# A recommendation kernel: one table fetched by single rows on two queues, weight loads spread between them, and a reordered tail

## The chip, the cores and the metric

The kernel runs on one core of one Trainium2 chip. Its time is device microseconds for one execution: a median of 236.08 us over three runs (235.92 to 236.24). The engines are PE (TensorE), DVE (VectorE), ACT (ScalarE), POOL (GpSimd) and SP (SyncE), and all transfers run on 16 DMA engines.

## The reference

For 512 samples, each of 26 tables (6250 rows of 128 float32) gives one row. The rows are summed, and they also feed a three-layer network:

```python
emb = jax.vmap(lambda tab, idx: tab[idx])(tables, cat_features)      # 26 x 512 x 128
emb_btd = jnp.transpose(emb, (1, 0, 2))
wide_num = jax.nn.relu(numerical @ w_wide + b_wide)                  # 13 numbers per sample
linear_output = jnp.sum(emb_btd, axis=1) + wide_num
x = jnp.concatenate([numerical, emb_btd.reshape(512, 26 * 128)], axis=1)
x = jax.nn.relu(x @ W1 + b1)                                         # 3341 -> 256
x = jax.nn.relu(x @ W2 + b2)                                         # 256 -> 128
return jax.nn.sigmoid(x @ W3 + b3 + linear_output)                   # 512 x 128
```

## The kernel before

A *tile* (t, c) is the 128 rows that table t gives for chunk c of 128 samples, four chunks in all. Every engine runs a list written out by hand, and semaphores tie the lists together. Tiles reach SBUF (`emb`) in three ways:

- **POOL** gathers most of them: `gather` (L299) is one indirect DMA for one tile. There are 97.
- **Rows apart.** SP fetches tiles (0, 2) and (0, 3), and ACT fetches tile (0, 1), row by row: `load_places` (L251) loads 32 row addresses into registers, `fetch_row` (L256) is one MOVE and one DMA of 512 bytes. SP does this in one go, after its four loads of W1 (L269). ACT does four rows in each step i of its loop (L622), which waits until part i is transposed (`turned`) and also loads a piece of table 12.
- **Table 12** is not gathered. It is read whole, in 13 pieces (`load_piece`, L243), as 49 blocks. For each block DVE marks which samples want which row (`hot_block`, L526), and PE multiplies block by marks into one bank (`pick_block`, L369).

The body of the work goes by 46 *parts*. A part is one table for two chunks. For part i PE transposes two tiles (`turn_part`, L344), DVE copies the result to SBUF (L546) and adds it to the running sum (L553), and PE multiplies it by W1 (`sum_part`, L358). PE's list has turn i+1, the blocks of step i, sum i. Table 0 is late: part 36 is (0, 0) with (0, 2), and part 43 is (0, 1) with (0, 3). Two parts stand behind it. In the float32 matmuls (L358, L369) one product is two passes on PE; a transpose is one. So a part is 2 passes of transposes, 4 of sums, and about 2.3 of blocks.

The tail treats tables 23 and 24 tile by tile (eight tiles, n = 0 to 7): PE transposes (L412), ACT copies (L633), DVE adds to the running sum (L587), PE multiplies by W1 (L421), and for each chunk follow the relus, layer 2 (L436), the turned running sum (`begin_total`, L431), layer 3 (L444), and the sigmoid (L642). `small_products` (L384, L387) are the 13-number part and the transposed biases. They stand behind part 1's sum, and the first picked block waits for them.

Of the kernel before, what the change touches and what calls it, by code (L numbers as in the profile page):

```python
# [11 lines left out]
P = 128  # L12
# [4 lines left out]
BY_SCALAR = [(0, 1)]  # L17
REGS = 32
ROWS_A_STEP = 4
# [3 lines left out]
W1_CUTS = [0, 2, 8, 17, 26]  # L23


def build(nc, num, cat, tables, w_wide, b_wide, W1, b1, W2, b2, W3, b3, out):
# [21 lines left out]
    assert all(t == 0 for t, c in BY_SYNC + BY_SCALAR)  # L48
# [8 lines left out]
    PICK_PARTS = (2, LAST - 8)  # L57
# [6 lines left out]
    def blocks(i):  # L64
        lo, hi = PICK_PARTS
        return range((i - lo) * BLOCKS // (hi - lo), (i + 1 - lo) * BLOCKS // (hi - lo)) if lo <= i < hi else range(0)
# [4 lines left out]
    BODY_TILES = [(0, 0)] + [tile for i in range(LAST) for tile in tiles(i) if tile != (0, 0) and not rows_apart(*tile)]  # L71

    assert BODY_TILES[1] == (1, 0)

# [10 lines left out]
    with ctx:  # L85
# [25 lines left out]
        def total_of(c):  # L111
            return total[c % 2][:, 0:D]
# [12 lines left out]
        next_sum = sb("next_sum", [P, 1])  # L125
# [52 lines left out]
        wide_cols, vec_place = total[0][:, 0:CH], total[0][:, CH:CH + KH + 2]  # L178
# [44 lines left out]
        late_gathered = [sem(f"late_gathered{n}") for n in range(TILES)]  # L223
        late_turned = sem("late_turned")
# [38 lines left out]
        def _(sp):  # L263
            with nc.allow_non_contiguous_dma(reason="one index for each partition"):
                sp.dma_start(first_cat[:, :], cat[0:1, 0:P].rearrange("a p -> p a")).then_inc(first_loaded, 16)
                sp.dma_start(next_cat[:, :], cat[1:2, 0:P].rearrange("a p -> p a")).then_inc(next_loaded, 16)
            for i, loaded in enumerate(w1_loaded):
                lo, hi = W1_CUTS[i], W1_CUTS[i + 1]
                sp.dma_start(w1[:, lo:hi, :], W1[NUM + lo * D:NUM + hi * D, :].rearrange("(t d) n -> d t n", d=D)  # L269
                             ).then_inc(loaded, 16)  # L270
# [16 lines left out]
        def _(gp):  # L287
# [18 lines left out]
            gather(0, 0, first_row[:, :], gathered[part_of(0, 0)])  # L306
            gp.wait_ge(next_steps, 4)
            gather(1, 0, next_row[:, :], gathered[part_of(1, 0)])
# [8 lines left out]
        def _(pe):  # L317
# [44 lines left out]
            def pick_block(j):  # L362
                if j == 0:
                    pe.wait_ge(vecs_ready, 1)
# [27 lines left out]
            turn_part(0)  # L392
            for i in range(LAST):
# [6 lines left out]
                if i == PICK_PARTS[0] - 1:  # L400
                    small_products()
# [3 lines left out]
            def turn_tile(n):  # L405
# [4 lines left out]
                else:  # L410
                    pe.wait_ge(late_added, n - 1)
# [28 lines left out]
            def layer3(c):  # L440
                pe.wait_ge(h2_ready, c + 1)
                if c == 0:
# [6 lines left out]
            for c in range(CH):  # L449
                n = c * LATE  # L450
                turn_tile(n)
                if c == 0:
                    sum_part(LAST - 1)
                else:
                    sum_tile(n - 1)
                    begin_total(c - 1)
                if c >= 2:
                    layer3(c - 2)
                turn_tile(n + 1)
                sum_tile(n)  # L460
                if 1 <= c < CH - 1:
                    layer2(c - 1)
            sum_tile(TILES - 1)
            layer2(CH - 2)
            layer2(CH - 1)
            layer3(CH - 2)
            begin_total(CH - 1)
# [3 lines left out]
        def _(dve):  # L471
# [3 lines left out]

            dve.wait_ge(first_loaded, 16)
            nc.vector.tensor_scalar(first_lim[:, :], first_cat[:, :], float(-V), float(V - 1), ALU.max, ALU.min
# [4 lines left out]
            nc.vector.tensor_tensor(first_row[:, :], first_neg[:, :], first_lim[:, :], ALU.add  # L482
                                    ).then_inc(first_steps, 1)
# [6 lines left out]
            nc.vector.tensor_scalar(next_lim[:, :], next_cat[:, :], float(-V), float(V - 1), ALU.max, ALU.min  # L490
# [6 lines left out]
            nc.vector.tensor_tensor(next_sum[:, :], next_neg[:, :], next_lim[:, :], ALU.add).then_inc(next_steps, 1)  # L497
            dve.wait_ge(next_steps, 3)
            nc.vector.tensor_scalar(next_row[:, :], next_sum[:, :], float(V), None, ALU.add).then_inc(next_steps, 1)
# [40 lines left out]
            for j in blocks(PICK_PARTS[0]):  # L540
                hot_block(j)
            for i, (_, q) in enumerate(PARTS):
# [12 lines left out]
                if i == PICK_PARTS[0] - 1:  # L555
                    small_steps()
                if i >= PICK_PARTS[0]:
                    for j in blocks(i + 1):
                        hot_block(j)
                if i == PICK_PARTS[1] - 1:  # L560
# [119 lines left out]
```

## Time and profile before

| | |
|---|---|
| median of three runs | 236.08 us |
| the profiled execution's own time | 237.66 us |
| its span, first to last instruction | 235.9 us |
| PE / DVE / ACT / POOL busy | 126.2 / 76.9 / 6.2 / 93.1 us |
| mean granted TensorE clock | 0.841 |
| DMA packets, bytes | 11244, 14.06 MB |

Busy time counts no DMA issue, register load or semaphore, so SP, which only issues, shows none. "q" behind an engine's name (SPq, ACTq) is that engine's instruction queue. In the slices each digit is the busy share of 5.9 us. A chain of waits is followed back from the last instruction; "issue" in it is time for which the profile shows no releaser.

### The profile page before, as it was taken

What the parts mean: (1) busy time and instruction counts of PE and PEld (TensorE: products, weight loads), DVE (VectorE), ACT (ScalarE), POOL (GpSimd) and SP (SyncE); (2) the same over time, 40 slices, a digit from 0 to 9 for tenths busy, and PEclk for the clock granted to TensorE, in tenths of its full rate; (3) what the DMA queues carried; (4) which work ended last, traced back from release to release, by engine and by line L of the source; (5) the groups of instructions that cost most, each with busy time, mean ns of one, the idle gap of its engine ahead of it and who ended that gap; (6) DMA issues with size and microseconds to landing.
All of it is one profiled execution on the core that took longest, in us unless ns stands there. A gap on an engine that the chain in (4) does not pass through costs nothing.

```text
span 235.9 us, 2252 instructions
## 1 busy us (share of the span) xinstructions
PE 126.2 (54%) x476; PEld 82.6 (35%) x476; DVE 76.9 (33%) x182; ACT 6.2 (3%) x18; POOL 93.1 (39%) x106
## 2 busy tenths in 40 slices
PE   2638200059000700060002719999999999999695
PEld 0415100034000300030002206666666666667594
DVE  3150000033000200110003018677667666845352
ACT  0200000000000000000000000000000000000052
POOL 5777777777777777777771000000000000000000
PEclk9999999999855555575555667999999999999999
DMA  5997613565545443362422003400000000000001
GB/s 150 331 262 170 106 47 51 52 47 103 54 61 45 103 57 48 52 97 54 52 54 63 5 2 93 138 9 4 4 5 4 2 2 1 2 6 2 1 13 34
DMA packets 11244, 14.06 MB, mean 60 GB/s; under 512 B 3308, under 2 KB 8015, under 8 KB 11231
## 3 DMA queue, kind: packets, MB, share of 16 engines
q0 software_dynamic: 3104, 6.36, 20.7%
q1 hardware_dynamic: 4768, 3.80, 5.4%
q10 hardware_dynamic: 3359, 3.76, 5.2%
q8 instruction: 4, 0.07, 0.1%
q14 instruction: 9, 0.07, 0.1%
HBM read 13.65 MB, written 0.26 MB: 59 GB/s over the span
## 4 chain that ended last, share of the span: by engine, by line
SPq 57%; issue 34%; PE 5%; DMA 1%; DVE 1%; ACT 0%; DVEq 0%
SPq L256 50%; SPq L251 7%; PE first_layer L358 1%; PE first_layer L421 1%; DMA first_cat<-in_r_cat_features 1%; PE first_layer L436 1%; PE total L444 1%; DMA emb<-in_L_rec_tables 0%; PE total L431 0%; PE turn L412 0%; PE turn L344 0%; ACT y L642 0%; PE total L320 0%; DVE row_idx L503 0%; DVE cat_row L495 0%
## 5 line engine op out<-in xcount | busy, mean ns | idle before, releaser
L299 POOL DMA_INDIRECT emb<-in_L_rec_tables,row_idx x95 | 89.7, 944 | 29.0 <-issue 29.0
L358 PE MATMUL first_layer<-emb_t,w 128*128 128x256 f32 x184 | 54.4, 423 | 68.2 <-issue 61.3
L358 PEld LDWEIGHTS first_layer<-emb_t,w 128*128 128x128 f32 x184 | 37.6, 212 | 94.4 <-issue 81.8
L369 PE MATMUL total<-hot,block_rows 128*128 128x512 f32 (+1 forms) x98 | 53.8, 656 | 24.8 <-issue 24.8
L546 DVE COPY emb_t<-turn 128x256 f32<-128x256 f32 x46 | 19.4, 422 | 105.4 <-remote 78.3
L526 DVE TENSOR_SCALAR hot<-total,row_no 128x512 f32<-128x512 f32 x49 | 35.3, 742 | 0.0
L369 PEld LDWEIGHTS total<-hot,block_rows 128*128 128x128 f32 (+1 forms) x98 | 17.5, 211 | 32.0 <-issue 32.0
L344 PE MATMUL turn<-ident,emb 128*128 128x128 f32 x92 | 20.3, 304 | 9.0 <-DMA emb<-in_L_rec_tables,row_idx 5.5
L344 PEld LDWEIGHTS turn<-ident,emb 128*128 128x128 f32 x92 | 13.9, 156 | 16.3 <-DMA emb<-in_L_rec_tables,row_idx 6.6
L553 DVE TENSOR_TENSOR emb_sum<-turn,emb_sum 128x256 f32<-128x256 f32 x44 | 18.3, 415 | 0.0
L533 DVE TENSOR_SCALAR wide<-total,b_sb 128x4 f32<-128x4 f32 x1 | 0.2, 222 | 31.6 <-issue 31.6
L633 ACT COPY late_t<-turn 128x128 f32<-128x128 f32 x8 | 2.1, 264 | 219.2 <-PE turn L412 219.2
L421 PE MATMUL first_layer<-late_t,w 128*128 128x128 f32 x32 | 5.0, 280 | 0.1
L421 PEld LDWEIGHTS first_layer<-late_t,w 128*128 128x128 f32 x32 | 4.2, 191 | 0.4 <-ACT late_t L633 0.2
L334 PE MATMUL first_layer<-num_t,w_num 13*128 13x256 f32 x8 | 3.8, 649 | 0.8 <-DVE num_t L509 0.8
L587 DVE TENSOR_TENSOR emb_sum<-turn,emb_sum 128x128 f32<-128x128 f32 x8 | 2.3, 292 | 3.0 <-ACT late_t L633 2.9
L334 PEld LDWEIGHTS first_layer<-num_t,w_num 13*128 13x128 f32 x8 | 2.5, 325 | 1.8 <-DVE num_t L509 1.3
L513 DVE TENSOR_SCALAR pick_lim<-pick_cat 128x512 f32<-128x512 int32 x1 | 0.4, 427 | 7.6 <-DMA pick_cat<-in_r_cat_features 7.6
L320 PE MATMUL total<-ident,cat_row 104*128 104x104 f32 x1 | 0.4, 408 | 4.0 <-DVE cat_row L495 4.0
L436 PE MATMUL first_layer<-h,w 128*128 128x128 f32 x16 | 2.3, 278 | 0.0
L412 PE MATMUL turn<-ident,emb 128*128 128x128 f32 x8 | 2.2, 272 | 0.0
L436 PEld LDWEIGHTS first_layer<-h,w 128*128 128x128 f32 x16 | 2.1, 191 | 0.0
(54 smaller groups left out, 34.2 us busy)
## 6 DMA issues: line engine op xcount, KB each, us to landing
emb<-in_L_rec_tables SPq DMA_DIRECT2D x256, 0.5 KB
block_rows<-in_L_rec_tables ACTq DMA_DIRECT2D x12, 256.0 KB, 2.9
w<-in_L_rec_W SPq DMA_DIRECT2D x2, 1152.0 KB
emb<-in_L_rec_tables ACTq DMA_DIRECT2D x128, 0.5 KB
emb<-in_L_rec_tables,row_idx POOLq DMA_INDIRECT x95
w<-in_L_rec_W SPq DMA_DIRECT2D x1, 768.0 KB
w<-in_L_rec_W SPq DMA_DIRECT2D x1, 256.0 KB
pick_cat<-in_r_cat_features ACTq DMA_DIRECT2D x1, 256.0 KB
```

Source lines behind the costliest of these rows:

```text
L251: eng.load(regs, cat_byte[t * CH + c:t * CH + c + 1, lo:lo + REGS])
L256: eng.dma_start(emb[b:b + 1, t, c, :].bitcast(U8), row_bytes[t:t + 1, bass.ds(at, ROW)]).then_inc(fetched[t, c], 16)
L299: nc.gpsimd.indirect_dma_start(emb[:, t, c, :], None, rows, bass.IndirectOffsetOnAxis(ap=index, axis=0)).then_inc(landed, 16)
L334: nc.tensor.matmul(first_half(k, q), w1_num[:, chunk(k)], cols, start=True, stop=True)
L344: mm = nc.tensor.transpose(turn[i % 2][:, chunk(j)], emb[:, t, c, :], ident[:, :])
L358: mm = nc.tensor.matmul(first_half(k, q), w1[:, t, chunk(k)], emb_t[:, i % SLOTS, :], start=False, stop=False, skip_group_check=True)
L369: mm = nc.tensor.matmul(pick_bank[:, :], block_rows[0:n, j, :], hot[0:n, j % PICK_RING, :], start=(j == 0), stop=(j == PER))
L421: mm = nc.tensor.matmul(first_chunk(k, c), w1[:, LATE_TABLES[g], chunk(k)], late_t[:, n, :], start=False, stop=False, skip_group_check=True)
L436: mm = nc.tensor.matmul(second_chunk(c), w2[:, k, :], h1[:, k, chunk(c)], start=False, stop=False, skip_group_check=True)
L526: nc.vector.tensor_scalar(hot[:, j % PICK_RING, :], pick_row[:, :], row_no[:, j:j + 1], None, ALU.is_equal).then_inc(hot_ready, 1)
L546: nc.vector.tensor_copy(emb_t[:, i % SLOTS, :], turn[i % 2][:, 0:HW]).then_inc(copied, 1)
L553: nc.vector.tensor_tensor(emb_sum[:, q, :], turn[i % 2][:, 0:HW], emb_sum[:, q, :], ALU.add).then_inc(added, 1)
```

## The change

- ACT also fetches tile (0, 0): 256 rows on ACT, 256 on SP, 96 gathers on POOL. ACT's rows no longer wait for `turned`. It loads two pieces of table 12 before them and one more ahead of each 18 rows.
- W1 is loaded in nine DMAs instead of four: two (tables 0 to 4) at SP's start, one ahead of each of SP's first seven register loads.
- POOL begins with tiles (1, 0) and (1, 2), which together are part 0.
- `small_products` stand behind part 0's transposes, in another bank. Two picked blocks are done before part 1, and blocks go along from part 0 on.
- Part (0, 1) is the last of the 46.
- In the tail the body's sums of all four chunks are transposed together, before the first tile's product (`begin_totals`), and DVE adds the late tiles to them as they were gathered, without waiting for the transposes.

```diff
-BY_SCALAR = [(0, 1)]
+BY_SCALAR = [(0, 0), (0, 1)]
-ROWS_A_STEP = 4
+ROWS_A_PIECE = 18
+PIECES_AHEAD = 2
+BLOCKS_AHEAD = 2
-W1_CUTS = [0, 2, 8, 17, 26]
+W1_CUTS = [0, 2, 5, 8, 11, 14, 17, 20, 23, 26]
+W1_AHEAD = 2
-    PARTS += [(t, q) for t in OTHERS[-4:-1] for q in range(2)] + [(0, 1)]
-    PARTS += [(t, q) for t in OTHERS[-1:] for q in range(2)]
+    PARTS += [(t, q) for t in OTHERS[-4:] for q in range(2)] + [(0, 1)]
...
-    PICK_PARTS = (2, LAST - 8)
+    PICK_PARTS = LAST - 8
...
-            for i, loaded in enumerate(w1_loaded):
+            for i in range(W1_AHEAD):
+                load_w1(i)
+            cuts = iter(range(W1_AHEAD, len(w1_loaded)))
             sp.wait_ge(bytes_ready, 1)
             for t, c in BY_SYNC:
                 for lo in range(0, P, REGS):
+                    for i in itertools.islice(cuts, 1):
+                        load_w1(i)
                     regs = load_places(sp, t, c, lo)
...
+                if i == 1:
+                    pe.wait_ge(vecs_ready, 1)
...
             turn_part(0)
+            small_products()
+            for j in range(BLOCKS_AHEAD):
+                pick_block(j)
...
-            def begin_total(c):
-                pe.wait_ge(late_added, (c + 1) * LATE)
-                if c >= 2:
-                    pe.wait_ge(y_ready, c - 1)
-                nc.tensor.matmul(total_of(c), sum_chunk(c), ident[:, :], start=True, stop=False, skip_group_check=True)
+            def begin_totals():
+                pe.wait_ge(added, LAST)
+                for c in range(CH):
+                    mm = nc.tensor.matmul(total_of(c), sum_chunk(c), ident[:, :], start=(c < 2), stop=False,
+                                          skip_group_check=True)
+                mm.then_inc(totals_begun, 1)
...
             def add_tile(n):
                 c, g = divmod(n, LATE)
-                dve.wait_ge(late_copied, n + 1)
+                dve.wait_ge(totals_begun, 1)
+                if c >= 2:
+                    dve.wait_ge(y_ready, c - 1)
...
+                dve.wait_ge(late_gathered[n], 16)
+                nc.vector.tensor_tensor(total_of(c), total_of(c), emb[:, LATE_TABLES[g], c, :], ALU.add
...
+            for i in range(PIECES_AHEAD):
+                load_piece(act, i)
...
-            for i in range(LAST):
-                act.wait_ge(turned, i + 1)
-                if i < PIECES:
-                    load_piece(act, i)
-                for t, c, b in places[i * ROWS_A_STEP:(i + 1) * ROWS_A_STEP]:
-                    if b % REGS == 0:
-                        regs = load_places(act, t, c, b)
-                    fetch_row(act, regs.pop(0), t, c, b)
+            for i, (t, c, b) in enumerate(places):
+                piece, apart = divmod(i, ROWS_A_PIECE)
+                if apart == 0 and piece + PIECES_AHEAD < PIECES:
+                    load_piece(act, piece + PIECES_AHEAD)
+                if b % REGS == 0:
+                    regs = load_places(act, t, c, b)
+                fetch_row(act, regs.pop(0), t, c, b)
```

SP's list from its first instruction, before; w is W1, first_cat and next_cat are the indices of the first two gathers:

```order
L265 DMA first_cat<-in_r_cat_features 128x1
L266 DMA next_cat<-in_r_cat_features 128x1
L269 DMA w<-in_L_rec_W 128x2x256
L269 DMA w<-in_L_rec_W 128x6x256
L269 DMA w<-in_L_rec_W 128x9x256 x2
L251 TENSOR_LOAD cat_byte
L256 DMA emb<-in_L_rec_tables 1x512 x32
```

and in the changed kernel:

```order
L268 DMA first_cat<-in_r_cat_features 128x1
L269 DMA next_cat<-in_r_cat_features 128x1
L273 DMA w<-in_L_rec_W 128x2x256
L273 DMA w<-in_L_rec_W 128x3x256 x2
L254 TENSOR_LOAD cat_byte
L259 DMA emb<-in_L_rec_tables 1x512 x32
L273 DMA w<-in_L_rec_W 128x3x256
```

Eight of the 26 tables of W1 are now ahead of the first row; the other 18 come in six loads, one after each 32 rows.

ACT's list around its first rows, before (block_rows is a piece of table 12, cat_byte the row addresses):

```order
L614 DMA pick_cat<-in_r_cat_features 128x512
L617 ACT_TABLE_LOAD
L617 ACTIVATE table_warm<-ident 1x1
L243 DMA block_rows<-in_L_rec_tables 128x512
L251 TENSOR_LOAD cat_byte
L256 DMA emb<-in_L_rec_tables 1x512 x4
L243 DMA block_rows<-in_L_rec_tables 128x512
```

and in the changed kernel:

```order
L246 DMA block_rows<-in_L_rec_tables 128x512 x2
L636 ACT_TABLE_LOAD
L636 ACTIVATE table_warm<-ident 1x1
L246 DMA block_rows<-in_L_rec_tables 128x512
L254 TENSOR_LOAD cat_byte
L259 DMA emb<-in_L_rec_tables 1x512 x18
L246 DMA block_rows<-in_L_rec_tables 128x512
L259 DMA emb<-in_L_rec_tables 1x512 x14
```

Before, four rows stood behind each piece, and each piece behind a wait for `turned`. Now ACT's rows wait for nothing but the addresses.

PE's list from the last part's sum into the tail, before (late_t is a copied late tile, h the hidden layer):

```order
L358 MATMUL first_layer_1<-emb_t,w 128x256 x2
L412 MATMUL turn<-ident,emb 128x128
L421 MATMUL first_layer_0<-late_t,w 128x128 x2
L412 MATMUL turn<-ident,emb 128x128
L421 MATMUL first_layer_0<-late_t,w 128x128 x2
L431 MATMUL total<-ident,emb_sum 128x128
```

and in the changed kernel:

```order
L371 MATMUL first_layer_1<-emb_t,w 128x256 x2
L445 MATMUL total<-ident,emb_sum 128x128 x4
L435 MATMUL first_layer_0<-late_t,w 128x128 x2
L426 MATMUL turn<-ident,emb 128x128 x2
L435 MATMUL first_layer_0<-late_t,w 128x128 x2
L435 MATMUL first_layer_1<-late_t,w 128x128 x2
```

The four transposes of the sums (L445) now stand in front of the tail's first product. Before, one (L431) stood in each chunk's work.

## Rows read from the trace of the kernel before

**Rows 1.** The page's slices.

```profile
PE   2638200059000700060002719999999999999695
...
POOL 5777777777777777777771000000000000000000
PEclk9999999999855555575555667999999999999999
```

**Rows 2.** The chain that ended last, by line, from the page.

```profile
SPq L256 50%; SPq L251 7%; PE first_layer L358 1%; PE first_layer L421 1%; DMA first_cat<-in_r_cat_features 1%; PE first_layer L436 1%; PE total L444 1%; DMA emb<-in_L_rec_tables 0%; PE total L431 0%; PE turn L412 0%; PE turn L344 0%; ACT y
```

**Rows 3.** The chain in order of time: start us, us, what.

```profile
34.06 0.71 SPq L256
34.77 0.69 issue
...
75.50 0.70 SPq L251
...
140.96 0.23 SPq L256
141.19 0.04 issue
...
143.19 2.18 SPq L251
155.89 2.12 SPq L251
...
219.24 1.18 DMA emb<-in_L_rec_tables
```

**Rows 4.** DVE's timeline, 49 to 128 us: start, us, operation, idle before.

```profile
49.56 0.22 DVE L533 TENSOR_SCALAR wide<-total,b_sb 128x4 f32<-128x4 f32 x1 [31.62 <-issue]
55.11 0.42 DVE L546 COPY emb_t<-turn 128x256 f32<-128x256 f32 x1 [3.61 <-issue]
76.95 0.42 DVE L546 COPY emb_t<-turn 128x256 f32<-128x256 f32 x1 [19.77 <-remote]
99.49 0.43 DVE L546 COPY emb_t<-turn 128x256 f32<-128x256 f32 x1 [21.13 <-remote]
127.62 0.42 DVE L546 COPY emb_t<-turn 128x256 f32<-128x256 f32 x1 [26.73 <-remote]
```

**Rows 5.** PE's timeline, single stretches.

```profile
24.24 0.24 PE L387 MATMUL total<-ident,vec_rows 4*128 4x4 f32 x1
53.48 0.64 PE L344 MATMUL turn<-ident,emb 128*128 128x128 f32 x2
140.91 2.08 PE L358 MATMUL first_layer<-emb_t,w 128*128 128x256 f32 x4 [6.89 <-DVE emb_t L546]
144.69 1.03 PE L358 MATMUL first_layer<-emb_t,w 128*128 128x256 f32 x4
220.47 0.33 PE L344 MATMUL turn<-ident,emb 128*128 128x128 f32 x1 [2.50 <-DMA emb<-in_L_rec_tables]
```

**Rows 6.** ACT's timeline.

```profile
7.12 0.20 ACT L617 ACTIVATE table_warm<-ident 1x1 f32<-1x1 f32 x1
...
27.77 9.09 ACTq L256 DMA_DIRECT2D emb<-in_L_rec_tables  x4
55.10 0.37 ACTq L243 DMA_DIRECT2D block_rows<-in_L_rec_tables  x1
55.56 1.21 ACTq L256 DMA_DIRECT2D emb<-in_L_rec_tables  x4
```

**Rows 7.** ACT's loads of 32 addresses (L251): ns min/median/max, first and last start.

```profile
L251 ACTq TENSOR_LOAD <-cat_byte x4: 2133/2160/2253, 14.1 to 177.5; - x4
```

**Rows 8.** POOL's timeline, the second gather and the last.

```profile
4.98 0.94 POOL L299 DMA_INDIRECT emb<-in_L_rec_tables,next_row  x1 [0.30 <-issue]
123.70 0.94 POOL L299 DMA_INDIRECT emb<-in_L_rec_tables,row_idx  x1 [0.30 <-issue]
```

**Rows 9.** The chain from the last row on: start us, us, what.

```profile
221.88 0.87 PE first_layer L358 x4
224.92 0.45 PE first_layer L421 x4
225.98 0.22 PE total L431 x2
```

**Rows 10.** DMA packets in 0 to 20, 0 to 80 and 0 to 140.3 us.

```profile
DMA packets 5425, 4.85 MB, mean 243 GB/s; under 512 B 1294, under 2 KB 5006, under 8 KB 5425
DMA packets 7685, 9.19 MB, mean 115 GB/s; under 512 B 2198, under 2 KB 5955, under 8 KB 7682
DMA packets 9228, 12.16 MB, mean 87 GB/s; under 512 B 2861, under 2 KB 6649, under 8 KB 9225
```

More of the change, by code:

```diff
@@ L1 @@
+import itertools
 from contextlib import ExitStack
@@ L43, in build @@
     assert LATE == 2 and B == CH * P and D == P and H2 == P and KH == 2 and T * CH <= P and W1_CUTS[-1] == T
-    assert all(t == 0 for t, c in BY_SYNC + BY_SCALAR)
+    assert sorted(BY_SYNC + BY_SCALAR) == [(0, c) for c in range(CH)]
     OTHERS = [t for t in range(1, T) if t not in LATE_TABLES and t != PICK_TABLE]
     PARTS = [(t, q) for t in OTHERS[:-4] for q in range(2)] + [(0, 0)]
-    PARTS += [(t, q) for t in OTHERS[-4:-1] for q in range(2)] + [(0, 1)]
-    PARTS += [(t, q) for t in OTHERS[-1:] for q in range(2)]
+    PARTS += [(t, q) for t in OTHERS[-4:] for q in range(2)] + [(0, 1)]
     LAST = len(PARTS)
     assert HALF == 2 and LAST == (BODY - 1) * 2 and PARTS[0][1] == 0 and PARTS[1][1] == 1
-    PICK_PARTS = (2, LAST - 8)
+    PICK_PARTS = LAST - 8
     PICK_END = LAST - 7
@@ L64, in blocks @@
     def blocks(i):
-        lo, hi = PICK_PARTS
-        return range((i - lo) * BLOCKS // (hi - lo), (i + 1 - lo) * BLOCKS // (hi - lo)) if lo <= i < hi else range(0)
+        n = BLOCKS - BLOCKS_AHEAD
+        return range(BLOCKS_AHEAD + i * n // PICK_PARTS, BLOCKS_AHEAD + (i + 1) * n // PICK_PARTS) if i < PICK_PARTS else range(0)
     def rows_apart(t, c):
         return (t, c) in BY_SYNC + BY_SCALAR
-    BODY_TILES = [(0, 0)] + [tile for i in range(LAST) for tile in tiles(i) if tile != (0, 0) and not rows_apart(*tile)]
-    assert BODY_TILES[1] == (1, 0)
+    BODY_TILES = [tile for i in range(LAST) for tile in tiles(i) if not rows_apart(*tile)]
+    assert BODY_TILES[:2] == [(1, 0), (1, 2)]
     def part_of(t, c):
@@ L305, in _ @@
             gp.wait_ge(first_steps, 3)
-            gather(0, 0, first_row[:, :], gathered[part_of(0, 0)])
-            gp.wait_ge(next_steps, 4)
-            gather(1, 0, next_row[:, :], gathered[part_of(1, 0)])
+            gather(1, 0, first_row[:, :], gathered[part_of(1, 0)])
+            gp.wait_ge(next_steps, 3)
+            gather(1, 2, next_row[:, :], gathered[part_of(1, 2)])
             gp.wait_ge(rows_ready, 1)
@@ L441, in layer3 @@
                 pe.wait_ge(h2_ready, c + 1)
+                pe.wait_ge(late_added, (c + 1) * LATE)
                 if c == 0:
@@ L453, in _ @@
                     sum_part(LAST - 1)
+                    begin_totals()
                 else:
+                    if c >= 2:
+                        layer3(c - 2)
                     sum_tile(n - 1)
-                    begin_total(c - 1)
-                if c >= 2:
-                    layer3(c - 2)
+                sum_tile(n)
                 turn_tile(n + 1)
-                sum_tile(n)
-                if 1 <= c < CH - 1:
+                if c >= 1:
                     layer2(c - 1)
             sum_tile(TILES - 1)
-            layer2(CH - 2)
             layer2(CH - 1)
             layer3(CH - 2)
-            begin_total(CH - 1)
             layer3(CH - 1)
@@ L538, in small_steps @@
                 nc.vector.tensor_scalar(w3_wide[:, :], ones[:, :], w3_col, None, ALU.mult).then_inc(w3_ready, 1)
-            for j in blocks(PICK_PARTS[0]):
+            for j in range(BLOCKS_AHEAD):
+                hot_block(j)
+            small_steps()
+            for j in blocks(0):
                 hot_block(j)
@@ L554, in _ @@
                                             ).then_inc(added, 1)
[L555 to L560, printed above, removed]
+                for j in blocks(i + 1):
+                    hot_block(j)
+                if i == PICK_PARTS - 1:
                     dve.wait_ge(hot_used, BLOCKS)
```

46 lines of the change are left out of this document (21 added, 25 removed).

## The prediction

> **What bounds the kernel now.** I read the slices first [rows 1]. POOL works evenly until slice 22, but PE hardly works before slice 24 (about 140 us) and is then full to the end. Table gathers alone would not do that. The chain by line [rows 2] names SP's row fetches: 57% of the span on L256 and L251. The chain in order of time [rows 3] says how. Around 34 us each MOVE or DMA of SP takes 1.40 us with its gap (0.71 + 0.69), so a row takes 2.8 us; from 140.3 us on a DMA takes 0.23 and a row 0.32 us. The address loads at 75.5 and 143.2 us are 32 rows apart, those at 143.2 and 155.9 also: 67.7 us against 12.7. So there is a slow stretch, from about 10 to 140.3 us, and a fast rest, in which the last 192 rows take 219.24 - 143.2 = 76.0 us, 0.396 a row with its share of the loads. About 9 of the 64 rows before 143.2 fall behind 140.3, so some 55 are fetched by then.
>
> The slow stretch holds PE in the same way. The transposed biases start at 24.24 [rows 5], but DVE, which waits for them, goes on at 49.56 [rows 4]. DVE's copies of parts 3 to 6 start at 55.11, 76.95, 99.49 and 127.62. By PE's order 8 passes lie between the first two and 8 between the next: 21.84 / 8 = 2.73 and 22.54 / 8 = 2.82 us a pass, whatever its width. A pass is a weight load and a matmul, so this too is 1.4 us an instruction. ACT's rows show it once (27.77: four in 9.09 us) and after an idle time not (55.56: four in 1.21) [rows 6]: a few instructions go freely, a continuous stream doesn't.
>
> What makes the stretch end at 140.3? POOL issues 97 gathers at (123.70 - 4.98) / 95 = 1.25 us [rows 8], and two steps of 0.70 us for each of 97 make 135.8 us, from the first one at 3.6 to 139.4. I take that as the mechanism: each gather puts two of the 0.7 us steps into something all queues share, and it runs 15 us behind POOL. It is argued from one coincidence of numbers, not shown.
>
> After 140.3 PE works without a gap and SP fetches rows, and the two end nearly together: PE waits 2.50 us for the last row at 220.47 [rows 5]. The path is slow stretch, rows, two parts, tail.
>
> **Part by part.**
> *96 gathers.* One fewer: 1.4 us off the stretch, so 138.9.
> *SP.* Eight tables of W1 ahead of the rows instead of 26 leave the queue emptier, and about 3 us of quick rows fit in before the stretch: some 5 more rows, 5 x 0.40 = 2.0 us off. One W1 load falls in the stretch (half a row, +0.2), the stretch is shorter by half a row (+0.2), and five follow behind it at about 0.47 us, +2.4 (bounds: 0.37, a piece [rows 6], and 0.71). Last row: 219.2 - 1.4 - 2.0 + 0.2 + 0.2 + 2.4 = 218.6; landed 1.18 later [rows 3], 219.8.
> *ACT.* This is the step I think decides. ACT used to fetch 128 rows with slack; now it has 256, 11 pieces between them and 8 address loads. After its table load at 7.3 us come the pieces (0.4 each) and a load of 2.16 [rows 7], so rows start near 10.7. Some 7 go quickly. From 14.5 to 138.9 it does 124.4 / 1.4 = 89 instructions: 2 pieces, 1 load and 43 rows. Left at 138.9: 206 rows x 0.325 (four in 1.21 [rows 6]) = 67.0, six loads x 2.16 = 13.0, eight pieces x 0.40 = 3.2, together 83.2. Issued by 222.1, landed at 223.3, against 220.4 now: +2.9. Bounds: if ACT keeps the quick pace for 10 more rows, -4; if its rows get only every second step because SP and ACT now both stream, 22 rows fewer, +7.
> *PE in the body.* Its passes in the stretch number the same; small products and picked blocks come a little earlier, and a block is the pass that costs most outside (about 1 us saved). PE reaches the last part near 217.5 and waits there about 5.8 us. So everything that PE saves in the body, and the earlier blocks with it, is hidden by the rows. W1's pieces are there in time: tables 11 to 13 are issued near 141 us, and PE, at two parts a table and 2.06 us a part, wants them about 25 us later.
> *Part (0, 1) last.* Two parts fewer behind the last row: 2 x (0.87 + 0.22) = -2.2 [rows 9].
> *Body's sums turned once.* Eight passes now stand ahead of the first late product, 4 x 0.22 = +0.9, and as many go from the tail, -0.9. Two waits that they covered come open, for ACT's copy of tile 1 and for the last relus, 0.5 to 1.2 us; DVE's adds leave the chain of copies. I take +0.4 for the tail in all (bounds -1.0, +1.5).
> *PE's clock.* After the wait of 6.9 us at 134 us four passes take 2.08 us [rows 5], and 1.03 us at 144.7: 1.2 against 2.4 GHz. The wait of 2.50 us at 218 was followed by 0.87 us for four [rows 9], full speed. The new wait of 5.8 us lies between. If the clock falls, some 4 us of passes run at half speed, +1.9; if not, 0. I take +0.4.
> The Trainium skill (TensorE: Matmul & The Clock Gate, HAM oscillation) says that PE gaps waiting for DMA slow the clock for the work behind them. By that rule the sum would take the +1.9 whole; the wait of 2.50 us here did not do it.
> Sum on the profiled span: 235.9 + 2.9 - 2.2 + 0.4 + 0.4 = 237.4, so +1.5. The profiled execution itself took 237.66 around its span of 235.9, the median is 236.08; the difference is put on the median: 237.6.
>
> **Rivals.**
> *B, ACT keeps up with SP.* If ACT's rows get through the stretch like SP's, the last row lands at 219.8 instead of 223.3 and the wait at the end is short: 237.6 - 3.5 = 234.1. For it: the four rows at 55.56 went freely. Against it: those at 27.77 did not, and now there is no idle time to recover in.
> *C, the stretch comes from the burst of packets at the start, not from the gathers. Faster, and by far.* 5425 packets in the first 20 us, 9228 by 140.3 [rows 10]: 66 a us on the average. If something works off a queue of packets at that rate, the queue is empty when the packets issued equal 66 t. The change takes 18 tables x 128 = 2304 packets of W1 out of the start. At 80 us 7685 - 2304 = 5381 are issued against 5280: the stretch ends near 83 us. Then SP, with some 32 rows done, needs 224 x 0.396 + 2.8 = 91 us and ACT about the same: last rows at 175, tail 15, 190; since W1, rows and pieces now come all together, some slow pace returns: 195 (185 to 215). It decides if the stretch ends before 120 us. For it: the slow pace starts while W1 streams in, and it goes on for 14 us after the last gather. Against it: the pace stays at 0.70 us to the last step, though the packets of the 16 engines would not run out together.
> The Trainium skill (NOTIFIC — the notification-queue block, Overflow: three behaviours) says that the block that records instructions and DMA packets pushes back on its producers rather than lose a record inside. That would be a form of C; nothing in this trace shows the block itself.
> *D, row streams themselves feed the stretch.* ACT's steady rows beside SP's would lengthen it: 128 more rows at two steps of 0.7 us, of which a tenth must show, 245 to 255. Against it: at 34 us, beside ACT's four rows, SP has the same pace [rows 3] as over its second 32 rows on the whole (67.7 us, 9 of them quick), when ACT hardly fetched.
>
> **How the numbers follow.** My forecast (A) 0.46, with its own range 234.8 to 241; B 0.15; C 0.28; D 0.11. The predicted time is A's 237.6. Range: A, B and the upper half of C make 0.46 + 0.15 + 0.15, with the lower part of D 0.80: 194 to 244. About 0.2% (0.5 us) is what can be told from no change. Faster: C 0.28, B 0.13, the low end of A 0.06: 0.47. Same: 0.06. Slower: 0.47.
>
> **What would show it.** The step pace of SP (1.40 an instruction) ending near 139 us confirms the first term; before 120, C. PE's last wait should be for a row that ACT fetched, 4 to 7 us long, with the wait's end at 222 to 225 us. If it is for SP's row, B. Five W1 loads of under 0.7 us between SP's rows behind the stretch; four passes behind the long wait at 0.87 us or at 1.7. From the first late product to the end 11 us as before. I am wrong if PE works before 120 us.

## The result, and the profile after

The changed kernel takes 243.78 us (median of 5 runs, 242.84 to 243.99). The kernel before took 236.08 us beside it (5 runs, 235.84 to 236.35). The ratio is 1.0319, with an interval of 1.0297 to 1.0341: 7.7 us slower, where I forecast 1.5 us slower. The direction was right, but I had given faster and slower the same chance, 0.47; the size was not. The profiled execution took 243.99 us, with a span of 242.1, which is 6.2 more than the span before. Medians below are over all executions of a run and ratios over those at the usual pace; one of six with tile (0, 0) by POOL took 383.4 us, which no run explains, and the median given for that run is that of the other five.

The slices of the page after, beside [rows 1]:

```profile
PE   2893060006002600500060099999999999990985
POOL 5777777777777777777730000000000000000000
PEclk9999555556655655575557569999999999998599
```

The shape is the same: PE hardly works up to slice 23 and is full behind it. New are the empty slice shortly before the end and the 8 and 5 in the clock, in that slice and the next. The chain by line has passed from SP [rows 2] to ACT:

```profile
ACTq L259 49%; ACTq L254 6%; ACTq L246 2%; PE first_layer L371 1%; PE first_layer L435 1%; PE first_layer L452 1%; PE total L461 1%; PE total L445 1%; DMA emb<-in_L_rec_tables 0%; DVE h L592 0%; ACT h L656 0%; PE turn L357 0%; ACTq L619 0%; ACT y L661 0%; DVE total L604 0%
```

The slow stretch is there, as in [rows 4]. DVE's timeline (start, us, operation, idle before it) shows the same copies some 22 us apart, and the first free one at 138.38:

```profile
54.24 0.42 DVE L564 COPY emb_t<-turn 128x256 f32<-128x256 f32 x1 [20.98 <-remote]
76.64 0.42 DVE L564 COPY emb_t<-turn 128x256 f32<-128x256 f32 x1 [20.98 <-issue]
...
138.38 0.42 DVE L564 COPY emb_t<-turn 128x256 f32<-128x256 f32 x1 [15.47 <-remote]
```

ACT's timeline shows 18 rows in 49.06 us inside the stretch and in 6.03 behind it (8.24 where a load of addresses lies among them):

```profile
37.40 49.06 ACTq L259 DMA_DIRECT2D emb<-in_L_rec_tables  x18
...
138.28 8.24 ACTq L259 DMA_DIRECT2D emb<-in_L_rec_tables  x18
...
147.01 6.03 ACTq L259 DMA_DIRECT2D emb<-in_L_rec_tables  x18
```

The end of the chain in order of time (start, us, what) has ACT's last load of addresses, the landing of its last row, and the first passes of PE behind it:

```profile
209.90 2.21 ACTq L254
...
222.55 1.21 DMA emb<-in_L_rec_tables
223.90 0.66 PE turn L357 x2
224.56 1.71 PE first_layer L371 x4
```

The last row has landed at 223.8 (222.55 + 1.21), and four passes take 1.71 us where they took 0.87 [rows 9]. PE's timeline gives the wait and the tail:

```profile
223.90 0.66 PE L357 MATMUL turn<-ident,emb 128*128 128x128 f32 x2 [5.87 <-DMA emb<-in_L_rec_tables]
...
227.98 1.60 PE L445 MATMUL total<-ident,emb_sum 128*128 128x128 f32 x8
229.42 0.61 PE L435 MATMUL first_layer<-late_t,w 128*128 128x128 f32 x4
...
232.65 0.49 PE L461 MATMUL total<-w_wide,h 128*128 128x128 f32 x2 [0.33 <-DVE h L592]
...
235.22 0.49 PE L461 MATMUL total<-w_wide,h 128*128 128x128 f32 x2 [0.52 <-DVE h L592]
```

The windows (busy us of PE, PEld, DVE, ACT, POOL, then the granted clock) date the fall of the clock:

```profile
218.00:222.00 4.00, 0.03 (x1) 0.00 (x0) 0.00 (x0) 0.00 (x0) 0.00 (x0) 1.00 0.01 3
222.00:224.00 2.00, 0.10 (x1) 0.13 (x2) 0.00 (x0) 0.00 (x0) 0.00 (x0) 0.57 0.01 1
224.00:226.00 2.00, 2.00 (x6) 1.60 (x7) 0.76 (x2) 0.00 (x0) 0.00 (x0) 0.50 0.00 0
226.00:228.00 2.00, 2.00 (x7) 1.58 (x6) 0.00 (x0) 0.27 (x1) 0.00 (x0) 0.50 0.00 0
228.00:230.00 2.00, 2.00 (x15) 2.00 (x13) 0.30 (x1) 0.00 (x0) 0.00 (x0) 0.72 0.00 0
```

It is at 0.50 (1.2 GHz) from before the end of the 5.87 us wait, and it is back at 2.4 GHz near 229. Behind that, PE works off a chunk in 235.22 - 232.65 = 2.57 us. DVE's timeline shows what stands in each chunk between two of PE's steps:

```profile
233.63 0.35 DVE L587 TENSOR_SCALAR h<-first_layer,vec_cols 128x128 f32<-128x128 f32 x1 [1.03 <-PE first_layer L435]
234.12 0.30 DVE L604 TENSOR_TENSOR total<-total,emb 128x128 f32<-128x128 f32 x1
234.62 0.30 DVE L604 TENSOR_TENSOR total<-total,emb 128x128 f32<-128x128 f32 x1 [0.20 <-DVE total L604]
234.83 0.34 DVE L592 TENSOR_SCALAR h<-first_layer,vec_cols 128x128 f32<-128x128 f32 x1
```

From the third chunk on, the first add also waits for ACT's sigmoid of the chunk two before, which frees its bank. ACT's timeline has it just ahead of the add at 234.12:

```profile
233.67 0.36 ACT L661 ACTIVATE y<-total,wide 128x128 f32<-128x128 f32 x1
```

### The profile page after: what moved, and what is told of

Same layout as the page of the kernel before. It is cut to its first block, busy times and chain, and to the rows that moved or that the text cites. A ratio compares the mean times of both kernels' runs of the same rounds, so it can differ in the third digit from the quotient of the medians.

```text
span 242.1 us, 2518 instructions
## 1 busy us (share of the span) xinstructions
PE 129.7 (54%) x476; PEld 85.1 (35%) x476; DVE 77.1 (32%) x181; ACT 6.2 (3%) x18; POOL 92.3 (38%) x105
## 3 DMA queue, kind: packets, MB, share of 16 engines
q0 software_dynamic: 3072, 6.30, 19.4%
## 4 chain that ended last, share of the span: by engine, by line
ACTq 59%; issue 32%; PE 5%; ACT 1%; DVE 1%; DMA 0%; DVEq 0%
ACTq L259 49%; ACTq L254 6%; ACTq L246 2%; PE first_layer L371 1%; PE first_layer L435 1%; PE first_layer L452 1%; PE total L461 1%; PE total L445 1%; DMA emb<-in_L_rec_tables 0%; DVE h L592 0%; ACT h L656 0%; PE turn L357 0%; ACTq L619 0%; ACT y L661 0%; DVE total L604 0%
## 5 line engine op out<-in xcount | busy, mean ns | idle before, releaser
L371 PE MATMUL first_layer<-emb_t,w 128*128 128x256 f32 x184 | 55.8, 432 | 96.7 <-issue 83.9
L371 PEld LDWEIGHTS first_layer<-emb_t,w 128*128 128x128 f32 x184 | 38.4, 216 | 124.3 <-issue 106.2
L382 PE MATMUL total<-hot,block_rows 128*128 128x512 f32 (+1 forms) x98 | 55.7, 672 | 0.0
L382 PEld LDWEIGHTS total<-hot,block_rows 128*128 128x128 f32 (+1 forms) x98 | 18.0, 219 | 5.9 <-issue 5.9
L652 ACT COPY late_t<-turn 128x128 f32<-128x128 f32 x8 | 2.0, 267 | 223.3 <-PE turn L426 223.3
L604 DVE TENSOR_TENSOR total<-total,emb 128x128 f32<-128x128 f32 x8 | 2.4, 298 | 5.1 <-PE total L445 4.3
L461 PE MATMUL total<-w_wide,h 128*128 128x128 f32 x8 | 1.9, 313 | 1.1 <-DVE h L592 1.1
L587 DVE TENSOR_SCALAR h<-first_layer,vec_cols 128x128 f32<-128x128 f32 x4 | 1.4, 351 | 3.1 <-PE first_layer L435 3.0
```

The source lines that it names most:

```text
L371: mm = nc.tensor.matmul(first_half(k, q), w1[:, t, chunk(k)], emb_t[:, i % SLOTS, :], start=False, stop=False, skip_group_check=True)
L382: mm = nc.tensor.matmul(pick_bank[:, :], block_rows[0:n, j, :], hot[0:n, j % PICK_RING, :], start=(j == 0), stop=(j == PER))
```

## The experiments

The runs were made in groups, each with the kernel before beside it. Beside the old tail, the filled wait, tile (0, 0) and W1 the kernel before took 236.44 us; beside the new tail, the 20 gathers left out and the blocks first 236.55. Differences to "the changed kernel" below are to its 243.78 us and so go across groups; it took 244.16 when it ran again. Theory at this point: the last row at 223.8, a tail made longer by its waits, and PE's clock each cost a part of the 7.7 us, and the stretch is 1.4 us a gather. Rivals: one of them alone, and a stretch made by packets.

**The old tail.**

```
-            def begin_totals():
+            def begin_total(c):
...
-                nc.vector.tensor_tensor(total_of(c), total_of(c), emb[:, LATE_TABLES[g], c, :], ALU.add
+                nc.vector.tensor_tensor(sum_chunk(c), late_turn(n), sum_chunk(c), ALU.add).then_inc(late_added, 1)
```

> The changed kernel, with the tail (order of PE, the body's sums turned chunk by chunk, both late rows added through the transposed copy) as it was before. Everything else as changed. Theory 1 (the new order makes PE wait for DVE and DVE for ACT, whatever the clock): eight passes come off from ahead of the first late product, -0.9 at full speed, and the rest of the tail is again limited by PE alone; last row of ACT still at 223.8, PE still at half speed for some 5 us: 241.5 to 242.5 us. Theory 2 (the tail is long only because PE's clock falls after the long wait): within 0.5 us of the changed kernel's 243.8, since as many passes are run at the low clock.

Measured: 241.48 us, 1.0217 of the kernel before (1.0174 to 1.026), so 2.3 less than the changed kernel. PE's timeline shows the chunks 2.0 us apart, and no wait behind the long one:

```profile
232.40 0.39 PE L458 MATMUL total<-w_wide,h 128*128 128x128 f32 x2
...
234.40 0.39 PE L458 MATMUL total<-w_wide,h 128*128 128x128 f32 x2
```

The clock fell here too, in a wait of 5.66 us. So theory 1: the order costs time of its own.

**The new tail alone**, in the kernel before (the same lines with + and - exchanged).

> The kernel before with the changed tail alone (body's sums turned once ahead of the first late product, late rows added by DVE from their gathered tiles, PE's new order). Theory 1 (the new order costs some 1.7 us of waits also at full clock): 237.6 to 238.8 us. Theory 2 (at full clock the orders cost the same, only the low clock made the new one long): within 0.5 us of the kernel before.

Measured: 239.30 us, 1.0122 (1.0098 to 1.0147), so +2.75, above what either theory gave (theory 1 up to 238.8). PE's passes are at full speed and the period of 2.57 us is there again:

```profile
227.87 0.49 PE L448 MATMUL total<-w_wide,h 128*128 128x128 f32 x2 [0.33 <-DVE h L579]
...
230.44 0.49 PE L448 MATMUL total<-w_wide,h 128*128 128x128 f32 x2 [0.52 <-DVE h L579]
```

**PE filled while it waits.**

```
+FILL = 6
...
+                if i == LAST - 1:
+                    pe.wait_ge(added, i - 1)
+                    for n in range(FILL):
+                        nc.tensor.matmul(total[n % 2][:, :], w1[:, 0, 0:P], block_rows[:, 0:4, :],
+                                         start=True, stop=True)
```

> The changed kernel, with six matmuls of 128 x 512 into a bank that is overwritten later, on PE just ahead of the last part, where it waits 5.9 us for the last row. Theory 1 (the wait lets the granted clock fall to 0.5 and that costs four turn passes 0.85 us, twice, begin_totals 0.5 and some of the late products): clock stays at 1.0, first late product 2.2 to 2.6 us earlier, 241.2 to 241.8 us. Theory 2 (the clock would not matter, the tail is bound by DVE and ACT): within 0.5 us of 243.8. If the six take longer than the wait, up to +0.5.

Measured: 241.83 us, 1.0239 (1.0198 to 1.0281), 2.0 less than the changed kernel though PE does more. PE's timeline:

```profile
218.34 5.31 PE L352 MATMUL total<-block_rows,w 128*128 128x512 f32 x12
223.59 0.41 PE L363 MATMUL turn<-ident,emb 128*128 128x128 f32 x2
223.83 1.03 PE L377 MATMUL first_layer<-emb_t,w 128*128 128x256 f32 x4
```

The four passes are at full speed again. The clock term is 2.0 us, as theory 1 had it.

**Tile (0, 0) by POOL.**

```
-BY_SCALAR = [(0, 0), (0, 1)]
+BY_SCALAR = [(0, 1)]
-ROWS_A_PIECE = 18
+ROWS_A_PIECE = 9
```

> The changed kernel, with tile (0, 0) gathered by POOL again (97 gathers) and ACT fetching one tile of rows. Theory 1 (slow stretch 1.4 us a gather; behind it SP's own rows end nearly as late as ACT's, with five loads of W1 between them): the stretch ends near 139.7, SP's last row lands near 222.7, time 242.8 (242 to 243.5). Theory 2 (only ACT's doubled rows made it slower): last row lands near 219.8, time 240 or less. If PE then waits under 3 us the clock stays up and another 2.4 us go: 240.4 by theory 1, 237.5 by theory 2.

Measured: 240.84 us, 1.0191 (1.0142 to 1.0241), 2.9 less. The first free copy of DVE is at 139.75, 1.4 us later, as 1.4 us a gather wants it. ACT issues its last row at 170.7, and the last row is now SP's. It lands at 222.15, nearer to theory 1 (222.7) than to theory 2 (219.8): with ACT's second tile gone, only 1.6 us come back. The time lies between theory 1 with the clock down (242.8) and with the clock up (240.4), and the windows show why:

```profile
222.00:224.00 2.00, 1.80 (x8) 1.55 (x9) 0.75 (x2) 0.27 (x1) 0.00 (x0) 0.86 0.00 0
224.00:226.00 2.00, 2.00 (x9) 1.73 (x8) 0.00 (x0) 0.00 (x0) 0.00 (x0) 0.50 0.00 0
226.00:228.00 2.00, 1.75 (x11) 1.52 (x11) 0.60 (x2) 0.43 (x2) 0.00 (x0) 0.78 0.00 0
```

PE had waited 2.80 us here. The clock fell 1.2 us after the wait had ended, with PE at work, and was low for some 3 us, where it was low for some 7 in the changed kernel. In the kernel before it did not fall after 2.50 [rows 5].

**W1 in four loads ahead of the rows.**

```
-W1_CUTS = [0, 2, 5, 8, 11, 14, 17, 20, 23, 26]
-W1_AHEAD = 2
+W1_CUTS = [0, 2, 8, 17, 26]
+W1_AHEAD = 4
```

> The changed kernel, with W1 loaded in four DMAs ahead of all rows, as before. Theory 1 (the slow stretch comes from the number of gathers): it ends at 138.3 as in the changed kernel, ACT's rows still end last, within 1 us of 243.8; SP's last row issues 1 to 3 us earlier than 220.4. Theory 2 (the stretch is the working off of packets, the first 20 us count): it ends 20 us or more later than at 138.3, and the time goes up by as much. Theory 3 (SP's W1 loads beside the rows slow ACT's rows): the last row lands 1 us or more earlier than 223.8, 241 to 242.5 us.

Measured: 244.09 us, 1.0333 (1.029 to 1.0376), as the changed kernel: theory 1. The packets of the first 20 us, of the changed kernel and then of this one:

```profile
DMA packets 3489, 3.13 MB, mean 156 GB/s; under 512 B 1361, under 2 KB 2785, under 8 KB 3489
```

```profile
DMA packets 5235, 4.84 MB, mean 242 GB/s; under 512 B 1299, under 2 KB 4587, under 8 KB 5235
...
138.22 0.42 DVE L564 COPY emb_t<-turn 128x256 f32<-128x256 f32 x1 [16.86 <-remote]
```

Half as many packets again, and the stretch ends at 138.22 against 138.38. Rival C, a stretch that works off the packets of the start, is refuted. SP's last row is issued at 218.33 instead of 220.13: W1 between the rows costs SP 1.8 us, which ACT hides.

**20 gathers left out.**

```
+LEFT_OUT = (16, 17, 18, 19, 20)
-                gather(t, c, column(t, c), gathered[part_of(t, c)])
+                if t not in LEFT_OUT:
+                    gather(t, c, column(t, c), gathered[part_of(t, c)])
```

> The changed kernel with the 20 gathers of tables 16 to 20 left out (76 gathers; the body turns table 1's tiles in their place, so the output is not the reference's; every pass, copy and row fetch stays). Theory 1 (the slow stretch lasts 1.4 us a gather): it ends near 138.3 - 28 = 110.3 us, the last row lands near 199, time 219 us (217 to 222). Theory 2 (the stretch has another source, such as the 768 row fetches or W1, blocks and rows together): it ends near 138 and the time stays within 1 us of 243.8.

Measured: 219.07 us (218.69 to 219.94), 0.9258 (0.9231 to 0.9286). DVE's first free copy:

```profile
110.66 0.42 DVE L566 COPY emb_t<-turn 128x256 f32<-128x256 f32 x1 [13.40 <-remote]
```

That is 27.7 us earlier for 20 gathers, 1.39 each, with all 512 rows (the expectation says 768), blocks and weights in place. POOL's last gather ends 12.3 us before that copy and 14.8 us before it in the changed kernel. So the stretch doesn't end a fixed time behind POOL; the backlog grows with every gather. Rival D had the row streams lengthen the stretch. With 128 more rows on ACT it ended at 138.38, earlier than the 140.43 of the kernel before. D falls too.

**20 gathers of half the rows.** The same, with those 20 gathers issued for 64 partitions each. The first time this kernel took 148.18 us, since the stretch was not there (below). The expectation then, and that of the second time:

> The changed kernel, with the 20 gathers of tables 16 to 20 fetching 64 rows each where they fetched 128 (the body turns table 1's tiles in their place, so the output is not the reference's). Theory 1 (the slow stretch counts gathers, 1.4 us each): it ends at 138.3, time within 1 us of 243.8. Theory 2 (it counts gathered rows, 11 ns each): it ends 14 us earlier, near 124, the last row lands about 12 us earlier and the time is 231 to 233 us.

> The changed kernel with 20 of the 96 gathers fetching 64 rows each, again (output not the reference's). If the slow stretch is there: theory 1 (it counts gathers) it ends at 138.3, time within 1 us of 243.8; theory 2 (it counts gathered rows, 11 ns each) it ends near 124, time 231 to 233 us.

Measured the second time: 244.67 us, 1.034 (1.0305 to 1.0374), DVE's first free copy at 138.65, against 138.66 for the changed kernel in the same group. The stretch counts gathers, not the rows or the bytes they fetch. But the page of this run has as many packets in the gathers' queue as that of the changed kernel:

```profile
q0 software_dynamic: 3072, 5.64, 16.7%
```

There it is 3072 packets with 6.30 MB, so 32 a gather in both. Whether each gather or each of its 32 packets holds the engines no run separates.

**The changed kernel again**, in the group of that run and the next two.

> The changed kernel itself, beside the others of this call. If the slow stretch is there (the kernel before at about 236 us): 243.8. If it is not (the kernel before at 134 us): theory 1 (ACT's 256 rows end last, as in the run with 20 gathers halved): 147 to 149 us, 10% slower. Theory 2 (without the stretch the change does what POOL's fewer gathers give): 133 us.

Measured: 244.16 us, 1.0327 (1.0288 to 1.0367), the kernel before 236.79. PE waited 5.24 us for the last row, and the granted clock was low from 223.8 to 227.2, some 3 us and not 7.

**Part (0, 1) last, alone**, in the kernel before.

```
-    PARTS += [(t, q) for t in OTHERS[-4:-1] for q in range(2)] + [(0, 1)]
-    PARTS += [(t, q) for t in OTHERS[-1:] for q in range(2)]
+    PARTS += [(t, q) for t in OTHERS[-4:] for q in range(2)] + [(0, 1)]
```

> The kernel before, with part (0, 1) as the last of the body and nothing else. Two parts of 1.09 us come off from behind SP's last row, so PE waits 4.7 us for it where it waited 2.5. Theory 1 (a wait of that length lets the granted clock fall, which takes back some 2 us): within 1 us of the kernel before, and PE at 0.5 behind the wait. Theory 2 (it falls only after waits nearer 6 us): 2.2 us less than the kernel before.

> The kernel before with part (0, 1) last, again. If the slow stretch is there: PE waits 4.7 us for SP's last row where it waited 2.5. Theory 1 (such a wait lets the granted clock fall and takes some 2 us back): within 1 us of the kernel before, PE at 0.5 behind the wait. Theory 2 (the clock stays): 2.2 us less. If the stretch is not there: no difference, as measured (0.9975).

Measured with the stretch: 235.26 us, 0.9933 (0.9894 to 0.9972), 1.5 less. My expectation had the wait the wrong way round: two parts that move ahead of the wait fill it and don't lengthen it. PE's timeline has no wait left:

```profile
219.01 0.38 PE L343 MATMUL turn<-ident,emb 128*128 128x128 f32 x2
219.23 1.03 PE L357 MATMUL first_layer<-emb_t,w 128*128 128x256 f32 x4
220.09 0.38 PE L343 MATMUL turn<-ident,emb 128*128 128x128 f32 x2
```

So it says nothing of the clock. It also says how long the wait usually is: the two parts are 2.2 us, and only 1.5 came back. The wait of 2.50 us [rows 5] is that of one execution, which at 237.66 us was 1.3 us above the slowest of the five. In the run of the new tail alone, whose body is that of the kernel before, PE waited 1.33 us. Without the stretch the ratio was 0.9975 (0.9939 to 1.0011), no difference.

**Three things back together**: the old tail, tile (0, 0) by POOL, three matmuls in the wait.

> The changed kernel with three things taken back together: the old tail, tile (0, 0) by POOL, and PE filled (three matmuls) while it waits for the last row. Theory 1 (these three are the whole loss, singly 2.3, 2.7 and 2.0, of which the second and third share about 1): 236.8 to 237.8 us. Theory 2 (something else in the change costs too, such as W1's loads between SP's rows, 1.8 us of SP's last row): 238.5 or more. Under 236 if the part order brings its 2.2 us once the clock stays up.

> The changed kernel with the old tail, tile (0, 0) by POOL and PE filled ahead of the last part, again. If the slow stretch is there: theory 1 (these three are the whole loss) 236.8 to 237.8 us, or under 236 if the part order brings its 2.2 us; theory 2 (W1 between SP's rows and the rest cost too) 238.5 or more.

Measured with the stretch: 237.70 us, 1.0034 (1.0004 to 1.0063), as theory 1. The three bring 6.5 of the 7.4 us by which the changed kernel was slower in that group. PE's wait is down to 0.55 us and its clock stays up, but the time under 236 that the part order was to bring did not come: the last row lands at 222.09, later than in the kernel before, and that takes it back. (Without the stretch: 136.61 us, 1.0146, where the kernel before took 134.19.)

**Blocks first.** A version built on the pace of the stretch: since PE does one pair of weight load and matmul in 2.8 us there, the pairs with the most columns should stand there.

```
-    PICK_PARTS = LAST - 8
+    PICK_PARTS = 1
-PIECES_AHEAD = 2
+PIECES_AHEAD = 13
-BY_SYNC = [(0, 2), (0, 3)]
-BY_SCALAR = [(0, 0), (0, 1)]
+BY_SYNC = [(0, 3)]
+BY_SCALAR = [(0, 1)]
...
-                    for i in itertools.islice(cuts, 1):
+                    for i in itertools.islice(cuts, 2):
```

> The changed kernel with all 49 picked blocks ahead of the parts (their 13 pieces loaded by ACT ahead of its rows), tiles (0, 0) and (0, 2) by POOL (98 gathers), one tile of rows each on SP and ACT. Theory 1 (in the slow stretch a pass costs PE 2.8 us whatever its width, so the widest should stand there): stretch ends near 141.1, by then about 40 blocks are done, 9 are left at 0.87, 44 parts at 1.09, last part near 200, time 212 to 216 us. Theory 2 (a pass of 512 columns takes longer there, or DVE's steps for the blocks are held as well): 20 blocks or fewer by 141 us, 230 us or more. Theory 3 (rows bind as before): 236 or more.

> The same with the tail of the kernel before. No row is waited for at the end, so the clock stays up: Theory 1 (the new tail costs by its waits): 1.0 to 2.3 us less than the run with the blocks first and the new tail. Theory 2 (it costs only at the low clock): within 0.5 us of it.

Measured: 230.32 us (0.9718, 0.9681 to 0.9755) with the new tail and 227.71 us (0.9628, 0.9591 to 0.9664) with the old one. Both beat both kernels. The first is far from theory 1 (212 to 216) and at theory 2's 230 or more. I had counted a block as one pair, and PE's timeline says otherwise:

```profile
108.57 2.04 PE L381 MATMUL total<-hot,block_rows 128*128 128x512 f32 x2 [3.62 <-DVE hot L540]
114.08 2.08 PE L381 MATMUL total<-hot,block_rows 128*128 128x512 f32 x2 [3.46 <-DVE hot L540]
...
141.39 5.49 PE L381 MATMUL total<-hot,block_rows 128*128 128x512 f32 x6 [2.84 <-DVE hot L540]
```

A block has two matmuls with a load each (the x2), so PE's own pairs would take 2 x 2.8 = 5.6 us in the stretch: 5.51 between these two. But DVE's timeline has the same pace:

```profile
107.67 0.75 DVE L540 TENSOR_SCALAR hot<-total,row_no 128x512 f32<-128x512 f32 x1 [4.85 <-issue]
113.28 0.75 DVE L540 TENSOR_SCALAR hot<-total,row_no 128x512 f32<-128x512 f32 x1 [4.85 <-remote]
```

Each block starts as its marks are ready (107.67 + 0.75 against 108.57), and DVE is never a block ahead of PE, though it has six buffers for marks. So DVE's steps were held as well, as theory 2 had it. Which of the two kept the block at 5.6 us this run doesn't separate; either way 26 blocks, not 40, were done when the stretch ended at 141.4. The tails differ by 2.6 us at full clock, near the 2.75 of the run of the new tail alone.

**Rows of three tiles on both queues**, the blocks first and the old tail, 97 gathers, twice, both times without the stretch.

```
+SHARED = [(0, 2)]
+            for t, c in SHARED + BY_SYNC:
+                for lo in range(0, P // 2 if (t, c) in SHARED else P, REGS):
```

> The run with the blocks first and the old tail (227.7 us), with tile (0, 2) fetched by rows again, half by SP and half by ACT: 97 gathers, 192 rows on each of the two. Theory 1 (PE is bound by what is left when the stretch ends, 1.4 us a gather): 226.3 us, the rows of both end near 195. Theory 2 (rows on two queues beside each other bind): 228 or more.

> The kernel with the blocks first, the old tail and tile (0, 2) by rows, half by SP and half by ACT (97 gathers), again. If the slow stretch is there: theory 1 (PE is bound by what is left when the stretch ends, 1.4 us a gather) 1.4 us less than with 98 gathers, 226.3; theory 2 (row fetches of 192 on each queue bind) 228 or more. If it is not there: 134.2 as measured.

> The kernel with the blocks first, the old tail and 98 gathers, beside the one with 97. If the slow stretch is there: 227.7 as measured. If it is not there: bound by POOL's gathers at 1.25 us each, one more than there, 135.4.

Measured: 134.22 us (0.9993, 0.9948 to 1.0037), and the second time 134.67 (1.0045) beside 135.36 (1.013) for the 98 gathers, with the kernel before at 133.92. What it does with the stretch stays open. Without the stretch the 98 gathers with the blocks first, the best version with it, are 1.3% slower than the kernel before: POOL is the bound there, and each gather counts.

## Why the prediction was off, step by step

- **The stretch, 1.4 us a gather (forecast to end at 138.9).** Right: 138.4. Argued from one coincidence then, it now has four counts: DVE's first free copy is at 110.7 with 76 gathers, at 138.2 to 138.7 with 96 and at 139.8 to 140.4 with 97, and the first free block at 141.4 and 142.3 with 98. Rivals C and D, 0.39 of the chance, are refuted. What it is that all engines share stays open.
- **ACT decides, last row landed at 223.3.** Right: 223.8, with ACT at 2.8 us a row inside the stretch (18 rows in 49.06 us) as forecast. Rival B is refuted: PE's last wait is for ACT's row.
- **SP, last row landed at 219.8.** 1.5 us short: it was issued at 220.13 where I had 218.6. Taking W1 out of the front and putting it between the rows, +0.6 by my terms (-2.0 + 0.2 + 2.4), costs 1.8. This made ACT's doubling look dearer than it is: tile (0, 0) back on POOL moves the last row only from 223.76 to 222.15.
- **Part (0, 1) last, -2.2.** In the kernel before it brings 1.5, as much as there is wait to fill. In the changed one the two parts fill part of a longer wait, so the term stands as I took it; no run takes it back alone.
- **The tail, +0.4 (bounds -1.0 and +1.5).** This is the step that failed. It measured +2.3 taken out of the changed kernel and +2.75 put into the one before, outside my bounds. From the first late product to the end it takes 12.7 us (229.42 to 242.1), where my sign was 11. I had priced two waits that come open once. But the new order closes a loop in the later chunks. Layer 3's pass waits for DVE's second relu (0.33, 0.52 and 0.22 us); this stands behind two adds of 0.30 us with a gap between them; these stand behind the first relu, which waits 1.03 us for PE's late products, and behind ACT's sigmoid; and the late products stand behind layer 3's pass. A chunk takes 2.57 us instead of 2.0, and PE had no such wait at all in the old order. That the order as a whole costs this is shown by three pairs of runs; how much of it is the order of the engines' lists, and how much the adds into the bank that the sigmoid must free first, no run separates.
- **PE's clock, +0.4 taken between 0 and +1.9.** It is the second miss: filling the wait gives 2.0, just above my upper end. I had weighted that end low because a wait of 2.50 us had done nothing. Nor was the wait of 6.9 us a clean case of a fall: in the kernel before the clock was at 0.50 ahead of it too, from 128 to 134 us. The rule I cited (the Trainium skill, TensorE: Matmul & The Clock Gate, HAM oscillation) pointed the right way: the trace agrees, and its sum, with +1.9 taken whole, would have been 239.1. The length of the one wait doesn't tell how much. The clock stayed up at 1.33 and 2.50 us, was low for some 3 us at 2.80 and at 5.24, and for some 7 at 5.46, 5.66, 5.87, 5.96 and 8.11. Where other waits stood close ahead it fell at shorter ones: in a wait of 2.41 (98 gathers, no stretch), and in this one of 1.57 us, which began 1.3 us after a wait of 1.35 had ended (20 halved gathers, no stretch):

```profile
115.22 0.69 PE L365 MATMUL turn<-ident,emb 128*128 128x128 f32 x2 [1.57 <-DMA emb<-in_L_rec_tables,row_idx]
115.70 1.91 PE L379 MATMUL first_layer<-emb_t,w 128*128 128x256 f32 x4
```

- **The sum.** On the spans: last row +3.3 (223.76 against 220.42), two parts fewer -2.2, clock +2.0, tail +2.75 make +5.9; measured are +6.2. The medians differ by 7.7, as the profiled execution of the kernel before was 1.6 us above its median. PE's wait ended at 220.47 in it and at 219.58 in the run of the new tail alone; taken from there the last row costs 0.9 more. Some 0.9 of the 7.7 stays open. Taken back together, tail, clock and tile (0, 0) bring 6.5, singly 2.3 + 2.0 + 2.9 = 7.2: the third holds some of the second.
- **The range.** 243.78 us lies outside the range of my own forecast, 234.8 to 241. The whole range, 194 to 244, holds it only by an upper end set for rival D, which is refuted; that is luck.

## What to carry to other kernels

Write down for each engine what stands ahead of each step of the last chunks, once for every chunk and not once for the tail: a producer that waits for its consumer's engine makes a loop, and its price is what it adds to the period times the chunks. Price a wait on the path also by what the clock does behind it; one that grows from 2.5 to 5.9 us cost 2.0 us more than its length, and work that only fills it gave this back. Don't read it off the length alone: the clock also fell in shorter waits that followed others. And where engines are held to a pace by instruction, put the instructions that do most there, counting on every engine that takes part what the hardware executes, not what the code names.

## What the runs showed of the hardware

The whole slow stretch is not a property of the kernel alone. The groups behind the result ran on four chips. On two of them, in three groups, the kernel before took 236.4 to 236.8 us; on the other two, in one group each, it took 134.19 and 133.92. Nothing else was changed. There, part (0, 1) last in the kernel before has these slices and this chain:

```profile
PE   0590289999999999999998998999999999999992
...
POOL 3777777787787787777777877877877777778500
...
POOL emb L298 63%; DMA emb<-in_L_rec_tables,row_idx 3%; PE first_layer L420 3%; PE first_layer L357 2%; DMA first_cat<-in_r_cat_features 2%; PE first_layer L435 1%; PE total L443 1%; PE turn L411 1%; PE total L430 1%; PE turn L343 0%; ACT y L641 0%; DVE first_row L481 0%; DVE first_lim L476 0%; DVE first_neg L478 0%
```

POOL's gathers have the same 1.25 us cadence, but PE works from the sixth slice on almost without a gap, and POOL is the bound. A row of SP, with its share of the address loads, takes 35.20 / 77 = 0.46 us in the midst of the gathers:

```profile
9.97 35.20 SPq L255 DMA_DIRECT2D emb<-in_L_rec_tables  x77
```

So gathers are not slow by themselves; on two of four chips each of them also held every other engine for two steps of 0.70 us, and the backlog ran 15 us behind POOL. What differs between these chips no run shows; only one of them was used in two groups, with the stretch in both, so that it goes with the chip is likely and not shown. Every execution here has a span and a granted clock of its own, so all of them were recorded, and no run shows whether the stretch is there without recording. The changed kernel itself was not run on the quick ones. Its form with 20 halved gathers was, with 148.18 us (1.0982, 1.0879 to 1.1085): there too ACT's rows end last. Its chain shows that the last one, issued at 117.48, lands only 11.9 us later, for which PE waits (start, us, what):

```profile
117.48 11.88 DMA emb<-in_L_rec_tables
...
129.50 0.41 PE turn L365 x2
```
